# Two attention layers on 32x32 tiles of TensorE, with 32x32 block transposes on VectorE

## Chip, cores and metric

The kernel runs on one core of a Trainium2 chip. The metric is the device time in microseconds. The kernel before has a median of 1524.22 us over three runs (1521.26 to 1524.74).

## What is computed

128 sequences of 64 tokens with 128 features go through four layers, each with a context of the same shape:

```python
# layer 0: causal attention (key < query; row 0 is zero), 16 heads of 8
q, k, v = query @ Wq + bq, key @ Wk + bk, values @ Wv + bv     # split into heads
attn = softmax(where(j < i, q @ k.T / sqrt(8), -1e30)); attn[:, :, 0, :] = 0
x = layer_norm(query + (attn @ v) @ Wo + bo)
x = layer_norm(x + relu(x @ W1 + b1) @ W2 + b2)
# layer 1: the same heads, no mask, no norm
x = x + softmax(q @ k.T / sqrt(8)) @ v @ Wo + bo
x = x + gelu(x @ W1 + b1) @ W2 + b2
# layer 2: gated fusion with the pooled context, then layer norm
# layer 3: RMS norm, 16 heads of 64
x = x + softmax(split(normed @ wq) @ split(ctx @ wk).T) @ split(ctx @ wv) @ wo
```

All is float32. Some products are made in three passes of a rounded format instead: a matrix is held as `high`, its rounded copy, and `low`, the rest, and high x high, high x low and low x high are summed (`split_mm`).

## The kernel before, in words

The work is cut into 16 groups of 8 sequences (512 tokens). Features lie on the 128 partitions, tokens in the free dimension, so that a tile of a group is 128x512. One head of 8 features takes 8 partitions. `PLAN` lists, for each engine, the steps of a group with a place in time; `PLANS` has own lists for the first two and the last two groups. `program` shifts a group's list by `TURN` and merges all groups by these numbers. The numbers set an order and nothing else: each engine runs its steps in it, and `Signal` gives the semaphore value that a step waits for. Steps of neighbouring groups alternate therefore. `BANKS` names the PSUM bank of every tile (8 banks of 128x512), `EMPTIED_BY` the step that frees it.

Names of steps: `q`, `k`, `v` are projections. `S.l.u` are the scores of layer l (0 or 1) and quad u (4 sequences), in four banks, one for each strip t of 32 partitions. `max` takes the largest score of each row (VectorE), `shift` subtracts it (TensorE, with `negmax` as weights), `exp` is ScalarE's, `sum` and a reciprocal VectorE's, `norm` the multiplication by it on GpSimd. `PT` transposes the normed probabilities on TensorE in four blocks of 128x128 per strip (line 740, `cst,prob`), `probT` copies them out of PSUM on ScalarE (line 1031). `O` multiplies them with the values, `ctx` picks each head's own part out of `O`'s banks into `aT` (lines 1280 and 1287), `o` is the output projection and `attout` adds the residual.

A head has only 8 rows, while a tile of TensorE takes 32 rows or more. So operands are masked: `Qm` holds the queries twice, each copy with other heads set to zero (ScalarE, line 1014), `Km` the keys twice (VectorE, line 1243), `Vm` the values twice (VectorE, line 1254), and one matmul of `S` (32 rows, 128 columns of weights, 128 moving columns) gives four heads' scores, 16 matmuls per quad. `O` has 64x32 tiles, 32 matmuls of 128 moving columns per quad, in two banks.

`h` and `f` are the two products of the feed-forward part; `h` is plain float32 here. `lnT`, `stats`, `rstd`, `z`, `lnF`, `ln_out` are the norms (transposes at line 740 with `fT` or `z`), `y_gamma`, `y_beta`, `square`, `yn`, `yn_high`, `yn_low` lead from layer 2 to layer 3. Steps with a 3 belong to the last layer; its probabilities go through `PT3` and `prob3T`, also with `cst,prob` at line 740. `out` adds layer 3's result into `y`, the last step of a group on VectorE (line 1416); SP stores `y` and loads the next group.

In the profile all matmuls but the transposes are of line 731. A plain float32 matmul leaves two records.

```python
rows = slice(32 * t, 32 * t + 32)
last = mm(blocks[t][:, s // 2, :, s % 2, :], Qm[l][rows, b].rearrange("p a q -> p (a q)"),
          Km[l][rows, b], start=(l == 1 and s == 0))
```

## Time and profile before

| | |
|---|---|
| median of 3 runs | 1524.22 us (1521.26 to 1524.74) |
| profiled execution | 1523.22 us |
| its span | 1521.7 us |
| TensorE busy | 1418.5 us, 93% |
| VectorE busy | 1080.6 us, 71% |
| ScalarE busy | 977.0 us, 64% |
| GpSimd busy | 488.1 us, 32% |
| DMA | 20.02 MB, mean 13 GB/s |

The span goes from the first to the last instruction; 1.5 us of the execution lie around it. Busy times of an engine are shares of the span. A mean of one operation is its own duration; where operations of one kind follow each other, the next starts before the last has ended, so that the distance of two starts is shorter than the duration. In the timeline a row joins neighbouring operations of one kind.

### The profile page before, as it was taken

Reading aid. Unit: us, or ns where it says so; the run is one execution under the profiler, and the core shown is the slowest. Engines: PE = TensorE matmul, PEld = TensorE weight load, DVE = VectorE, ACT = ScalarE, POOL = GpSimd, SP = SyncE. Lnnn points to the kernel's source line nnn. Section 1 sums busy time; section 2 is a strip of 40 time slices with the busy share of each in tenths; the row PEclk is TensorE's granted clock in tenths of the full one; section 3 lists DMA queues with packets and bytes.
Section 4 is the critical chain, followed back from the end, with each engine's and each line's share of the span. In section 5 each row is a group of like instructions: output and inputs, shape, how many; then the busy total and the mean of one; then the engine's idle time right before and its main releaser. Section 6 shows DMA issues by size and latency. Waiting matters only on the chain.

```text
span 1521.7 us, 48865 instructions
## 1 busy us (share of the span) xinstructions
PE 1418.5 (93%) x20325; PEld 1030.3 (68%) x20325; DVE 1080.6 (71%) x2644; ACT 977.0 (64%) x1877; POOL 488.1 (32%) x522
## 2 busy tenths in 40 slices
PE   4779999999999999999999999999999999999987
PEld 3455766767676676767667676776767667676756
DVE  4558778677786867778676777867687785776743
ACT  2355767667676766767576676767667676665654
POOL 2132523315242341524224252332424233152402
PEclk9999999999999999999999999999999999999998
DMA  4000000000000000000000000000000000000000
GB/s 141 15 2 15 3 8 16 9 16 2 22 3 9 16 9 16 3 22 3 9 16 9 16 3 22 3 9 16 9 16 3 9 16 9 2 3 8 3 8 9
DMA packets 27798, 20.02 MB, mean 13 GB/s; under 512 B 1088, under 2 KB 27200, under 8 KB 27328
## 3 DMA queue, kind: packets, MB, share of 16 engines
q1 hardware_dynamic: 27584, 16.90, 3.8%
q8 instruction: 167, 2.74, 0.8%
q14 instruction: 47, 0.39, 0.1%
HBM read 12.70 MB, written 4.19 MB: 11 GB/s over the span
## 4 chain that ended last, share of the span: by engine, by line
PE 76%; DVE 10%; POOL 5%; ACT 4%; issue 4%; DMA 0%; SPq 0%; ACTq 0%; DVEq 0%
PE bank L731 63%; PE bank L740 13%; DVE negmax L1261 2%; POOL prob L1157 2%; DVE sums L1408 2%; ACT prob L1096 1%; POOL rstd L1144 1%; DVE z L1319 1%; ACT probT L1031 1%; DVE negmax L1402 1%; DVE stats L1305 1%; POOL prob L1137 1%; POOL var_eps L1141 1%; POOL w_low L1128 0%; DVE mv L1310 0%
## 5 line engine op out<-in xcount | busy, mean ns | idle before, releaser
L1137 POOL TENSOR_TENSOR prob<-prob,rinv 128x512 f32<-128x512 f32 x256 | 262.4, 1044 | 369.1 <-DVE rinv L1268 368.7
L740 PE MATMUL bank<-cst,prob 128*128 128x128 f32 x1536 | 221.5, 277 | 14.5 <-POOL prob L1157 9.6
L740 PEld LDWEIGHTS bank<-cst,prob 128*128 128x128 f32 x1536 | 173.9, 141 | 62.5 <-issue 32.7
L1031 ACT ACTIVATE probT<-bank 128x512 f32<-128x512 f32 x256 | 143.8, 598 | 110.3 <-PE bank L740 109.4
L1261 DVE TENSOR_REDUCE negmax<-bank 128x8 bf16<-128x512 f32 x256 | 159.0, 680 | 70.7 <-PE bank L731 70.6
L1157 POOL TENSOR_TENSOR prob<-prob,rinv 128x512 f32<-128x512 f32 x128 | 132.5, 1042 | 230.0 <-DVE rinv L1412 229.7
L1024 ACT ACTIVATE prob<-bank 128x512 f32<-128x512 f32 x256 | 142.0, 608 | 80.3 <-PE bank L731 80.0
L1266 DVE TENSOR_REDUCE sums<-prob 128x8 f32<-128x512 f32 x256 | 169.2, 661 | 12.9 <-ACT prob L1024 11.0
L731 PE MATMUL bank<-negmax,ident_b 128*128 128x512 bf16 x384 | 129.6, 389 | 14.1 <-DVE negmax L1261 8.3
L731 PE MATMUL bank<-wt,Q 128*128 128x128 f32 x1024 | 126.1, 277 | 0.0
L1096 ACT ACTIVATE prob<-bank,rms_rows 128x256 f32<-128x256 f32 x256 | 104.5, 483 | 30.8 <-PE bank L731 30.7
L731 PEld LDWEIGHTS bank<-wt,Q 128*128 128x128 f32 x1024 | 120.8, 192 | 4.4 <-issue 1.0
L731 PE MATMUL bank<-room,wt 128*128 128x512 f32 x256 | 123.3, 593 | 0.0
L1074 ACT ACTIVATE K<-bank 128x512 f32<-128x512 f32 x128 | 74.2, 605 | 51.4 <-PE bank L731 51.0
L1141 POOL TENSOR_TENSOR var_eps<-mv,ln_eps 128x4 f32<-128x4 f32 x48 | 15.0, 313 | 279.1 <-DVE mv L1310 279.1
L1402 DVE TENSOR_REDUCE negmax<-bank 128x8 bf16<-128x512 f32 x128 | 81.6, 659 | 30.1 <-PE bank L731 30.0
L1109 ACT ACTIVATE Q<-bank 128x512 f32<-128x512 f32 x128 | 71.8, 597 | 46.6 <-PE bank L731 46.6
L1280 DVE TENSOR_SCALAR half_ctx<-bank,cst,vec 128x126 f32<-128x126 f32 (+1 forms) x128 | 46.4, 402 | 75.8 <-PE bank L731 75.6
L731 PE MATMUL bank<-c_high,w_high 128*128 128x512 f32 x160 | 85.4, 534 | 10.8 <-POOL w_low L1128 9.4
L1408 DVE TENSOR_REDUCE sums<-prob 128x8 f32<-128x512 f32 x128 | 85.1, 665 | 10.6 <-ACT prob L1096 10.3
L1079 ACT ACTIVATE V<-bank 128x512 f32<-128x512 f32 x128 | 75.7, 598 | 24.8 <-PE bank L731 22.6
L1104 ACT ACTIVATE prob3T<-bank 128x512 f32<-128x512 f32 x128 | 73.7, 603 | 26.3 <-PE bank L740 25.2
(155 smaller groups left out, 2968.7 us busy)
## 6 DMA issues: line engine op xcount, KB each, us to landing
x_in<-in_x SPq DMA_DIRECT2D x16, 256.0 KB, 3.0
c_in<-in_ctx SPq DMA_DIRECT2D x16, 256.0 KB, 3.3
out<-y SPq DMA_DIRECT2D x16, 256.0 KB, 2.3
Q<-in_split_weights SPq DMA_DIRECT2D x1, 1536.0 KB, 9.1
wt<-in_weights SPq DMA_DIRECT2D x1, 1024.0 KB, 10.8
wt<-in_weights SPq DMA_DIRECT2D x1, 640.0 KB, 5.9
wt<-in_weights SPq DMA_DIRECT2D x4, 128.0 KB, 10.4
cst<-in_constants SPq DMA_DIRECT2D x1, 229.0 KB, 2.7
```

Source lines behind the costliest of these rows:

```text
L731: return nc.tensor.matmul(o, lhsT, rhs, start=start, stop=stop, skip_group_check=True)
L740: last = nc.tensor.transpose(o[:, k * P:(k + 1) * P], src(k), ident)
L1024: nc.scalar.activation(prob[l][:, t].rearrange("p c k -> p (c k)"), bank(g, "S", l, u, t)[:, :], ACT.Exp, scale=SCALE8).then_inc(exp_ready ...
L1031: nc.scalar.activation(probT[:, t].rearrange("p s q -> p (s q)"), bank(g, "PT", l, u, t)[:, :], ACT.Identity).then_inc(probT_ready.sem, 1)
L1079: nc.scalar.activation(V3[:, b // 2, b % 2].rearrange("p j d -> p (j d)"), bank(g, "v3", b)[:, :], ACT.Identity).then_inc(v3_ready.sem, 1)
L1096: last = nc.scalar.activation(prob3[:, m % 2, :, i, :].rearrange("p (t e) k -> p t e k", e=2)[:, :, e, :], bank(g, "S3", m, e)[:, 256 * i: ...
L1137: nc.gpsimd.tensor_tensor(pr, pr, ri, ALU.mult).then_inc(norm_ready.sem, 1)
L1157: nc.gpsimd.tensor_tensor(pr, pr, ri, ALU.mult).then_inc(norm3_ready.sem, 1)
L1261: nc.vector.tensor_reduce(negmax[l][:, t, :], bank(g, "S", l, u, t)[:, :].rearrange("p (c k) -> p c k", c=8), AX.X, ALU.max, negate=True). ...
L1266: nc.vector.tensor_reduce(sums[l][:, t, :], prob[l][:, t], AX.X, ALU.add).then_inc(sum_ready.sem, 1)
L1402: nc.vector.tensor_reduce(negmax3[:, m % 2, e, :], bank(g, "S3", m, e)[:, :].rearrange("p (c k) -> p c k", c=8), AX.X, ALU.max, negate=Tru ...
L1408: nc.vector.tensor_reduce(sums3[:, m % 2, 4 * h:4 * h + 4].rearrange("p j i -> p (j i)"), prob3[:, m % 2, 4 * h:4 * h + 4].rearrange("p j ...
```

## The change

- **Scores.** `Qm` is gone: `queries` holds the queries once. `Km` holds the keys four times, one copy for each head of a strip, with the keys of a sequence ordered by parity. A matmul of `S` has 32 rows and 32 query columns as weights and 256 moving columns, and its output goes to 32 partitions: 32x32 tiles, 32 matmuls per quad. The causal mask is laid out anew for it.
- **Probabilities.** `PT` and `probT` are gone. `turn` on VectorE transposes a strip, 128x512, in 32x32 blocks from SBUF to SBUF.
- **Output.** `V` holds the values once, without a mask. `O` has 32x32 tiles, 32 matmuls of 256 moving columns per quad, in four banks. `ctx` picks four heads instead of two, with eight operations instead of four.
- **Copies.** `km` and `vm` move from VectorE to ScalarE.
- **`h`** becomes a split product: `x_high` on ScalarE and `x_low` on GpSimd are new, the weights W1 are split in the beginning.
- **`yn`** is gone. `lnF` of layer 2 transposes `y`, after gamma and beta; `yn_high` reads PSUM.
- `PLAN`, `PLANS`, `TURN`, `TILES` and `BANKS` are new throughout.

```diff
@@ the order: two lines of it @@
-        S.0.0@342.4468 shift.0.0.3@346.9911 ...
-TURN = 89.7521
+        S.0.0@199.6828 shift.0.0.0@203.6223 ...
+TURN = 83.4887
@@ buffers @@
-        Qm = [room[l][:, 0:2 * TOK].rearrange("p (b a q) -> p b a q", b=GB, a=2) for l in range(2)]
-        Km = [room[l][:, 2 * TOK:].rearrange("p (b c k) -> p b c k", b=GB, c=2) for l in range(2)]
+        Km = [room[l][:, :].rearrange("p (b h k) -> p b h k", b=GB, h=QUAD) for l in range(2)]
+        queries = [sb(f"queries{l}", [P, GB, L]) for l in range(2)]
-        Vm = sb("Vm", [P, 2, GB // 2, 2, P])
+        V = sb("V", [P, 2, 2, 2, P])
-        probT = sb("probT", [P, QUAD, QUAD, P])
+        probT = sb("probT", [P, QUAD, 8, L])
@@ TensorE @@
-                    for s in range(QUAD):
-                        b = QUAD * u + s
-                        for t in range(QUAD):
-                            rows = slice(32 * t, 32 * t + 32)
-                            last = mm(blocks[t][:, s // 2, :, s % 2, :], Qm[l][rows, b].rearrange("p a q -> p (a q)"),
-                                      Km[l][rows, b], start=(l == 1 and s == 0))
+                    for n in range(2):
+                        for i in range(QUAD):
+                            b = QUAD * u + i
+                            for t in range(QUAD):
+                                rows = slice(32 * t, 32 * t + 32)
+                                last = mm(blocks[t][32 * i:32 * i + 32, :, n, :], queries[l][rows, b, 32 * n:32 * n + 32],
+                                          Km[l][rows, b], start=(l == 1 and n == 0))
...
-                elif kind == "PT":
-                    l, u, t = index
-                    pe.wait_ge(*norm_ready(g, l, u, t))
-                    pr = prob[l][:, t].rearrange("p c k -> p (c k)")
-                    transpose4(bank(g, "PT", l, u, t), lambda k: pr[:, k * P:(k + 1) * P]).then_inc(probT_filled.sem, 1)
                 elif kind == "O":
...
-                        pe.wait_ge(*probT_ready(g, l, u, t))
+                        pe.wait_ge(*turned(g, l, u, t))
...
                     for j in range(2):
-                        for k in range(2):
-                            for r in range(2):
-                                rows = slice(64 * r, 64 * r + 64)
-                                for t in range(QUAD):
-                                    cols = slice(32 * t, 32 * t + 32)
-                                    last = mm(bank(g, "O", l, u, r)[cols, j * P:(j + 1) * P],
-                                              Vm[rows, l, 2 * u + j, k, cols], probT[rows, t, 2 * j + k, :],
-                                              start=(j == 0 and k == 0))
+                        for i in range(QUAD):
+                            rows = slice(32 * i, 32 * i + 32)
+                            for t in range(QUAD):
+                                cols = slice(32 * t, 32 * t + 32)
+                                last = mm(where[i][cols, 0:2 * P], V[rows, u, j, l, cols], probT[rows, t, :, 32 * j:32 * j + 32],
+                                          start=(j == 0))
...
-                    mm(bank(g, "h", l, j)[:, :], w(f"W1_{l}", j * P), (x1T[0] if l == 0 else fT[1])[:, :])\
+                    split_mm(bank(g, "h", l, j)[:, :], w_split(f"W1_{l}", j * P), (x_high[:, :], x_low[:, :]))\
@@ ScalarE @@
+                    nc.scalar.activation(queries[l][:, :, :].rearrange("p b q -> p (b q)"), bank(g, "q", l)[:, :],
+                                         ACT.Identity, bias=v(f"bq{l}")).then_inc(qm_ready.sem, 1)
...
+                        nc.scalar.activation(w_high[:, rest], w_stage[:, rest], ACT.Identity).then_inc(high_rest, 1)
+                        act.wait_ge(split_last_loaded, 16)
+                        nc.scalar.activation(w_high[:, last], w1_stage, ACT.Identity).then_inc(high_last, 1)
+                elif kind == "km":
...
-                    for a in range(2):
-                        last = nc.scalar.activation(Qm[l][:, :, a, :], bank(g, "q", l)[:, :].rearrange("p (b q) -> p b q", b=GB),
-                                                    ACT.Identity, bias=bqm[:, l, a:a + 1], scale=c("m_a", a))
+                    for h in range(QUAD):
+                        last = nc.scalar.activation(Km[l][:, :, h, :].rearrange("p b (j k) -> p b j k", j=2), by_parity,
+                                                    ACT.Identity, bias=bkm[:, l, h:h + 1], scale=m_h[:, h:h + 1])
+                elif kind == "vm":
...
+                    nc.scalar.activation(V[:, u].rearrange("p j l f -> p (j l f)"), bank(g, "v", u)[:, :], ACT.Identity)\
...
                 elif kind == "exp":
+                    if u or g:
+                        act.wait_ge(*(turned(g, l, 0, t) if u else turned(g - 1, l, 1, t)))
...
+                elif kind == "x_high":
...
+                    nc.scalar.activation(x_high[:, :], (x1T[0] if l == 0 else fT[1])[:, :], ACT.Identity)\
@@ GpSimd @@
+                elif kind == "x_low":
+                    l, = index
+                    pool.wait_ge(*x_high_ready(g, l))
+                    nc.gpsimd.tensor_tensor(x_low[:, :], (x1T[0] if l == 0 else fT[1])[:, :], x_high[:, :], ALU.subtract)\
@@ VectorE @@
+                elif kind == "turn":
+                    l, u, t = index
+                    dve.wait_ge(*norm_ready(g, l, u, t))
+                    if (l, u, g) != FIRST_QUAD:
+                        dve.wait_ge(*ctx_filled(QUAD_BEFORE[l, u, g][2], *QUAD_BEFORE[l, u, g][:2], part=QUAD - 1))
+                    nc.vector.transpose(probT[:, t].rearrange("p c k -> p (c k)"), prob[l][:, t].rearrange("p c k -> p (c k)"))\
+                        .then_inc(turned.sem, 1)
...
+                    for h in range(QUAD):
+                        for d in range(2):
...
+                            if h == 0:
+                                dve.wait_ge(*ctx_filled(g, l, u, part=2 * d + 1))
+                                nc.vector.tensor_scalar(half, o, m_h[:, 0:1], v(f"bv{l}"), ALU.mult, ALU.add)\
+                                    .then_inc(half_ready.sem, 1)
+                                continue
+                            dve.wait_ge(*half_ready(g, l, u, part=2 * (h - 1) + d))
+                            if h < QUAD - 1:
+                                nc.vector.scalar_tensor_tensor(half, o, m_h[:, h:h + 1], half, ALU.mult, ALU.add)\
+                                    .then_inc(half_ready.sem, 1)
+                            else:
+                                at = QUAD * u + 2 * d
+                                nc.vector.scalar_tensor_tensor(aT[l][:, at:at + 2, q0:L], o, m_h[:, h:h + 1], half,
+                                                               ALU.mult, ALU.add).then_inc(ctx_ready.sem, 1)
```

How the order moves, at three places. First TensorE, around the `O` of the first quad of layer 1 in a group of the middle, before (`cst,prob` are transposes, `probT,Vm` is `O`, `room` alone is `S`):

```order
L731 MATMUL bank<-wt,Q 128x128 x8
L740 MATMUL bank<-cst,prob 128x128 x4
L731 MATMUL bank<-negmax,ident_b 128x512
L731 MATMUL bank<-prob3T,V 64x64 x32
L740 MATMUL bank<-cst,prob 128x128 x12
L731 MATMUL bank<-negmax,ident_b 128x512
L740 MATMUL bank<-cst,prob 128x128 x4
L731 MATMUL bank<-probT,Vm 32x128 x32
L731 MATMUL bank<-room 128x2x64 x16
```

The same place in the change (`probT,V` is `O`, `room,queries` is `S`):

```order
L728 MATMUL banks<-wt,Q 128x128 x8
L728 MATMUL banks<-negmax,ident_b 128x512 x2
L728 MATMUL banks<-probT,V 32x256 x32
L728 MATMUL banks<-wt,Q 128x128 x8
L737 MATMUL banks<-cst,prob 128x128 x8
L728 MATMUL banks<-prob3T,V 64x64 x32
L728 MATMUL banks<-room,queries 32x4x64 x32
```

Of the transposes only those of the last layer are left (two strips of four), and `O` now stands between products of the last layer.

Second VectorE, around the `ctx` of the same quad, before (line 1266 is `sum`, 1408 the last layer's, 1261 `max`):

```order
L1408 TENSOR_REDUCE sums<-prob 128x8
L1412 RECIPROCAL rinv<-sums 128x8
L1266 TENSOR_REDUCE sums<-prob 128x8
L1268 RECIPROCAL rinv<-sums 128x8
L1280 TENSOR_SCALAR half_ctx<-bank,cst,vec 128x128 x2
L1287 SCALAR_TENSOR_TENSOR aT<-bank,cst,half_ctx 128x2x64 x2
L1261 TENSOR_REDUCE negmax<-bank 128x8 x4
```

In the change (line 1273 is `sum`, 1425 the last layer's):

```order
L1273 TENSOR_REDUCE sums<-prob 128x8
L1275 RECIPROCAL rinv<-sums 128x8
L1419 TENSOR_REDUCE negmax<-banks 128x8 x2
L1282 STREAM_TRANSPOSE probT<-prob 128x512 x3
L1425 TENSOR_REDUCE sums<-prob 128x8
L1429 RECIPROCAL rinv<-sums 128x8
...
L1300 TENSOR_SCALAR half_ctx<-banks,m_h,vec 128x128 x2
L1305 SCALAR_TENSOR_TENSOR half_ctx<-banks,m_h,half_ctx 128x128 x4
L1309 SCALAR_TENSOR_TENSOR aT<-banks,m_h,half_ctx 128x128 x2
```

Transposes stand between the reductions, and four more operations between the first and the last of a `ctx`.

Third TensorE at the start of the program, before (rows from the `k` of the first group on; the second threesome is a `k3`):

```order
L731 MATMUL bank<-c_high,w_low 128x512
L731 MATMUL bank<-pooled,wt 128x8
L731 MATMUL bank<-c_high,w_high 128x512
L731 MATMUL bank<-c_low,w_high 128x512
L731 MATMUL bank<-c_high,w_low 128x512
L731 MATMUL bank<-causal_rows,causal_pick 128x8x32 x8
L731 MATMUL bank<-room 128x2x64 x16
```

In the change:

```order
L728 MATMUL banks<-c_high,w_high 128x512
L728 MATMUL banks<-c_low,w_high 128x512
L728 MATMUL banks<-c_high,w_low 128x512
L728 MATMUL banks<-causal_rows,causal_pick 128x4x64 x8
L728 MATMUL banks<-room,queries 32x4x64 x32
```

No `k3` stands ahead of the first `S`.

## Rows read from the trace of the kernel before

**Rows 1.** The page: span, and busy time of each engine.
```profile
span 1521.7 us, 48865 instructions
PE 1418.5 (93%) x20325; PEld 1030.3 (68%) x20325; DVE 1080.6 (71%) x2644; ACT 977.0 (64%) x1877; POOL 488.1 (32%) x522
```
**Rows 2.** Busy time by stretch: PE, PEld, DVE, ACT, POOL, then PEclk, DMA share, GB/s.
```profile
403.00:1301.00 898.00, 867.24 (x12691) 635.09 (x12690) 668.77 (x1621) 607.76 (x1168) 299.68 (x319) 1.00 0.04 11
```
**Rows 3.** Timeline of VectorE, the last step of groups 1 and 14: start, us.
```profile
200.15 0.69 DVE L1416 TENSOR_TENSOR y<-bank,y 128x512 f32<-128x512 f32 x1 [0.50 <-PE bank L731]
...
1371.23 0.69 DVE L1416 TENSOR_TENSOR y<-bank,y 128x512 f32<-128x512 f32 x1 [4.39 <-PE bank L731]
```
**Rows 4.** The page: the chain that ended last, by engine.
```profile
PE 76%; DVE 10%; POOL 5%; ACT 4%; issue 4%; DMA 0%; SPq 0%; ACTq 0%; DVEq 0%
```
**Rows 5.** Timeline of TensorE: one strip's transposes and what follows.
```profile
620.28 0.60 PE L740 MATMUL bank<-cst,prob 128*128 128x128 f32 x4
620.72 0.38 PE L731 MATMUL bank<-negmax,ident_b 128*128 128x512 bf16 x1
```
**Rows 6.** Timeline of TensorE: an `O`, an `S` and what follows.
```profile
624.63 1.15 PE L731 MATMUL bank<-probT,Vm 64*32 64x128 f32 x64 [0.34 <-ACT probT L1031]
625.71 1.17 PE L731 MATMUL bank<-room 32*128 32x128 f32 x32
626.82 0.66 PE L740 MATMUL bank<-cst,prob 128*128 128x128 f32 x4
```
**Rows 7.** Timeline of TensorE: a split product, then a plain one, of 512 columns.
```profile
601.93 0.39 PE L731 MATMUL bank<-yn_high,w_high 128*128 128x512 f32 x1
...
602.63 0.28 PE L731 MATMUL bank<-rms_own,cst 128*128 128x8 f32 x2
...
648.51 1.02 PE L731 MATMUL bank<-room,wt 128*128 128x512 f32 x2
649.38 0.60 PE L740 MATMUL bank<-cst,prob 128*128 128x128 f32 x4
```
**Rows 8.** Waits of TensorE from 403 to 1301 us: total, times, longest.
```profile
PE bank L740 <- POOL prob L1157: 6.4, 27, 0.3
...
PE bank L731 <- ACT probT L1031: 3.5, 10, 0.4
```
**Rows 9.** Groups of VectorE, whole span: busy us, mean ns, idle before.
```profile
L1243 DVE TENSOR_SCALAR room<-bank,vec,m_c 128x512 f32<-128x512 f32 x64 | 48.4, 797 | 5.1 <-PE bank L731 5.1
L1254 DVE TENSOR_TENSOR Vm<-bank,m_vc 128x512 f32<-128x512 f32 x64 | 41.0, 683 | 35.4 <-PE bank L731 35.4
L1327 DVE TENSOR_TENSOR room<-x1T,gv 128x512 f32<-128x512 f32 x16 | 18.3, 1142 | 0.5
L1380 DVE TENSOR_SCALAR ynT<-bank,yn_scale 128x512 f32<-128x512 f32 x16 | 12.9, 804 | 4.9 <-PE bank L740 4.8
```
**Rows 10.** Timeline of VectorE: a `ctx` of a quad, then four maxima.
```profile
625.87 0.73 DVE L1280 TENSOR_SCALAR half_ctx<-bank,cst,vec 128x128 f32<-128x128 f32 x2 [1.31 <-PE bank L731]
626.52 0.60 DVE L1287 SCALAR_TENSOR_TENSOR aT<-bank,cst,half_ctx 128x128 f32<-128x128 f32 x2
627.04 2.47 DVE L1261 TENSOR_REDUCE negmax<-bank 128x8 bf16<-128x512 f32 x4
```
**Rows 11.** Groups of ScalarE, whole span.
```profile
L1031 ACT ACTIVATE probT<-bank 128x512 f32<-128x512 f32 x256 | 143.8, 598 | 110.3 <-PE bank L740 109.4
L1014 ACT ACTIVATE room<-bank,bqm,cst 128x512 f32<-128x512 f32 x64 | 46.2, 773 | 18.9 <-PE bank L731 18.2
L1063 ACT ACTIVATE yn_high<-ynT 128x512 fp32r<-128x512 f32 x16 | 10.1, 630 | 11.8 <-DVE ynT L1380 11.8
```
**Rows 12.** Group of GpSimd, whole span.
```profile
L1137 POOL TENSOR_TENSOR prob<-prob,rinv 128x512 f32<-128x512 f32 x256 | 262.4, 1044 | 369.1 <-DVE rinv L1268 368.7
```
**Rows 13.** Timeline of TensorE: the first `k3`.
```profile
26.01 0.80 PE L731 MATMUL bank<-c_high,w_high 128*128 128x512 f32 x1 [9.41 <-POOL w_low L1128]
```

766 lines of the change are left out of this document (367 added, 399 removed), and 9 rows, old and new, of the table BANKS.

## Prediction

> **What bounds the kernel now.** I read the totals of the page first. TensorE is busy for 1418.5 of 1521.7 us, VectorE for 1080.6 [rows 1]. Then the stretches, since a share over the whole span mixes start, middle and end: from 403 to 1301 us TensorE is busy for 867.24 of 898 us (96.6%) at a granted clock of 1.00, VectorE for 74.5%, ScalarE for 67.7%, GpSimd for 33.4% [rows 2]. Next the distance between groups: the sum into `y` that closes a group starts at 200.15 and, thirteen groups later, at 1371.23, so a group takes 90.1 us [rows 3]. Per group this is 87.0 us of TensorE and 3.1 us in which it idles, 67.1 of VectorE, 61.0 of ScalarE, 30.1 of GpSimd. The chain of waits agrees: 76% of it is TensorE, 10% VectorE [rows 4]. So the kernel is a stream of sixteen groups behind one full engine. A microsecond of TensorE work taken out of a group is worth up to 15 us, since fifteen steps lie between sixteen groups; work on the others is free as long as they don't become late for TensorE, which obeys a written order.
>
> **What TensorE loses and gains.** The four transposes of one quarter of a quad take from 620.28 to 620.72, 0.44 us [rows 5]. There are 16 such quarters in a group (2 layers, 2 quads, 4 row strips), all removed: 7.0 us.
>
> The products of `h` change from plain to split form. A plain one of 512 columns (one matmul, two records) takes from 648.51 to 649.38, 0.87 us; a split one (three matmuls) from 601.93 to 602.63, 0.70 us [rows 7]. Eight per group save 1.4 us.
>
> The scores `S` and the products `O` are the unknown. The trace has no 32x32 tiles. It has `S` as 16 matmuls of 128 columns, four tiles side by side, 1.11 us; and `O` as 32 matmuls of 128 columns, eight tiles side by side, 1.08 us [rows 6]. Matmuls times columns over tiles is 512 in both, and both take the same time. Now each is 32 matmuls of 256 columns on sixteen tiles: 512 again. `O` already issues its 64 records in 1.08 us, so the number of instructions isn't new either. I take 1.1 us, no change. Bounds: below, nothing is won (512 columns through a tile remain); above, only eight tiles work side by side (2.2 us) or four (4.4 us). I am nearest to the `O` row, which shares the number of records, the 32 columns of each weight tile and the many tiles.
>
> Here a rule weighs against the change. The Trainium skill (TensorE: Matmul & The Clock Gate, "Measured speedup vs the span model") gives 3.07 for four row tiles and 10.6 for sixteen, not 16. Four tiles agree with the trace: sixteen matmuls of 128 columns are four of 0.87 us, 3.48, and took 1.11. By the page the new block would be sixteen times 0.87 over 10.6, an estimated 1.31 us.
>
> TensorE then needs 87.0 - 7.0 - 1.4 = 78.6 us per group.
>
> **VectorE.** Removed per group: the masked keys (48.4 us in all), the masked values (41.0) and `ynT` (12.9) [rows 9], over 16 groups 6.4 us. Added: 16 transposes of 128x512. No row has one. Other operations that stream 512 elements step by 0.62 us (four `negmax` in 2.47) [rows 10]; the slowest row of that size is the product into `room` at 1.14 us [rows 9]. I take 0.62, as the transpose has one input and no broadcast: 9.9 us. 0.62 to 1.14 is the range, so 9.9 to 18.2. Nothing speaks for less than 0.5 us.
>
> `ctx` has eight operations for each quad instead of four. Two `tensor_scalar` take 0.65 us (625.87 to 626.52), two `scalar_tensor_tensor` 0.52 [rows 10]. Before: 1.17. Now two and six: 0.65 + 6 x 0.26 = 2.2. Four quads: 4.2 us more. `yn_low` reads PSUM now, 0.1. Sum: 67.1 - 6.4 + 9.9 + 4.2 + 0.1 = 74.9 us (83.2 with slow transposes). VectorE goes from 74% to near 90% of a group and is the second full engine.
>
> **ScalarE and GpSimd.** ScalarE loses 143.8 us of `probT` and 46.2 of masked queries [rows 11], 11.9 per group. It gains ten bias copies by the latter's row (0.72 each, two `qm` and eight in two `km`), two of `vm` by the former's (0.56) and two `x_high` (0.63): 9.6. So 58.7 us, no bound. What waits behind the four copies of a `km` is `S`; in the table `km.1` stands some twenty us before `S.1.0`, so this is hidden but in the first group. GpSimd gains two `x_low` by the row of its 512-element product (1.03) [rows 12]: 32.2 us.
>
> **Moves.** In the order of TensorE the run of `cst,prob` between the `negmax` and the `O` is gone; `O` waits for four transposes of VectorE in its place. They stand behind sums of layers 3 and 1 and ahead of a `ctx`, so a late `norm` on GpSimd now holds up VectorE, where before it held TensorE: TensorE idled 6.4 us for the last layer's `norm` and 3.5 for `probT` in the whole stretch [rows 8]. The second goes. A quad's latency falls by 0.44 + 0.56 and rises by 0.62 + 1.05; `x_high` and `x_low` put 1.7 us ahead of each `h`. In the middle neighbouring groups cover this. `exp` must now wait until the same strip of the quad before is turned, which the order has ahead of it. SP's queue gets one load more, at the start, and its waits stay.
>
> **The period.** 78.6 plus the old 3.1 of idle is 81.7. VectorE's free time would shrink from 23.0 to under 7 us there, and its work comes in bursts (four maxima, four sums, four transposes), each 2.5 us and more, in a fixed order. With a third of the slack, I let TensorE's idle nearly double, by 2.5, and take 84.2, where VectorE has 9 us free: no growth would need perfect cover, and growth by 8.4 would mean that VectorE's bursts are covered by nothing. This is the softest step. It keeps 5.9 of the 8.4 us.
>
> **Start and end.** TensorE idles 9.41 us until 26.01, for the low halves of the weights of `k3`, ahead of the first `S` [rows 13]. Now the first `S` stands ahead of any `k3`; it waits for ScalarE, which rounds these weights (and the new 1024 columns) ahead of `km`. I take 5 us of the 9.4 as won. The longer chains of the first and last group (two `h`, four `ctx`) cost 4 us.
>
> **Sum.** 15 x 5.9 = 88.5; plus 5, less 4: 89.5 us. From the profiled execution's 1523.2 us this gives 1433.7, so **1434 us**. The median of the runs shown, 1524.2, is 1 us above that execution, inside their spread of 3.5.
>
> **Rivals.**
> 1. *Sixteen tiles lose more than eight.* Each of the eight blocks (`S` and `O`) takes 1.3 us instead of 1.1, as extra staggering of 16 starts; 1.6 per group, 25 in all: 1459. Against: four and eight tiles cost the same [rows 6]. Chance 0.10. (This is the page's 10.6 as a mechanism; by it the time is the same 1459.)
> 2. *VectorE becomes the bound.* Transposes at the 1.14 us of the slowest row make 83.2 us of work; with its short gaps and a few waits the group takes about 87.5. Gain 15 x 2.6 + 1 = 40: 1483. For: no row of a transpose, and 90% is already little slack. Chance 0.13.
> 3. *Slower: column tiles of one row strip don't run side by side.* Then a block of `S` or `O` goes by eight or four. With eight, 2.2 us: 78.6 + 8.8 + 3.1 = 90.5 per group, about 1529. With four, 4.4 us: 105 + 3.1 = 108, about 1793. It decides once a block takes over 1.1 + 5.9/8 = 1.84 us. For: the four strips read four streams each, which no row shows. Against: `O` has four column tiles and two row tiles, with a stream of their own each, at the full rate. Chance 0.09.
> 4. *The change doesn't take the transposes out.* Excluded: the order has none left, and 32 transposes by VectorE between the reductions.
>
> **How the numbers follow.** The forecast has 0.66. Its own range goes from 1400 (idle nearly unchanged; all of it unchanged gives 1396) to 1465 (5 us more idle than taken, less than the 8.4 removed). Rivals 1 and 2 lie at 1459 and 1483; reaching to 1488 leaves out rival 3, part of rival 2 and a little at both ends of the forecast: 2 in 10. 0.3% is 4.6 us, about what a measurement of this kernel can tell from none. Faster by more: 0.66 + 0.10 + 0.11 = 0.87; the same, 0.03, from a bad rival 2 or a mild rival 3; slower 0.10, rival 3 and what I haven't thought of.
>
> **What would show it.** Right: no `cst,prob` but the last layer's 512 transposes; blocks `banks<-room,queries` and `banks<-probT,V` of 1.1 us from start to next start; `probT<-prob` near 0.62 to 0.68 us; groups 84 us apart; TensorE still over 92% busy and VectorE near 89%. Wrong: a block over 1.8 us, a transpose over 1.1, or chains in which VectorE has a third; `O` idle behind `turn`, with GpSimd's `prob` as what VectorE waits for, would say that the idle was mis-sized and not the work.

## The result, and the profile after it

The changed kernel takes 1526.32 us (median of 20 runs, 1522.39 to 1530.63), the kernel before 1523.13 on the same chip (1516.29 to 1525.42): ratio 1.0024, 95% interval 1.0013 to 1.0035. That is no difference, or one of a quarter of a per cent in the wrong direction, where I had forecast 1434 us. The profiled execution has a span of 1523.1 us. Two runs further down stand apart from the others of their kernel, one of six of `few_before` (1519.41 us, with a granted clock of 0.94 where the others have 0.99) and one of four of `placed_few2` (2531.77 us); the time given for `placed_few2` and the second ratio given for `few_before` leave them out.

The page of the changed kernel, the stretch from 403 to 1301 us (PE, PEld, DVE, ACT, POOL, PEclk, DMA share, GB/s) and the chain of waits answer to [rows 1, 2, 4]:

```profile
span 1523.1 us, 51571 instructions
PE 1359.0 (89%) x21477; PEld 926.2 (61%) x21477; DVE 1197.4 (79%) x3005; ACT 928.3 (61%) x1782; POOL 519.9 (34%) x555
...
PE 62%; DVE 20%; ACT 9%; issue 7%; POOL 2%; DMA 0%; SPq 0%; DVEq 0%; ACTq 0%
```
```profile
403.00:1301.00 898.00, 828.66 (x13402) 567.67 (x13401) 740.73 (x1853) 573.19 (x1105) 318.14 (x340) 1.00 0.04 11
```

TensorE did get less to do: busy for 828.66 us of the stretch instead of 867.24. But it idles for 69.3 us instead of 30.8, and the groups pass no faster. VectorE and ScalarE are where I had put them. In the chain VectorE, ScalarE and `issue` have taken what TensorE lost.

The sixteen sums into `y` of the changed kernel start at 189.92, 287.02, 375.43, 464.56, 553.47, 642.38, 731.88, 820.79, 911.13, 1001.26, 1092.84, 1184.69, 1276.69, 1367.10, 1447.94 and 1519.33 us. So the first group is 10.2 us earlier than before [rows 3], the next thirteen take 90.55 us each instead of 90.08, 6.1 us more in all, and the last two take 152.2 us instead of 146.8 (1371.2 to 1518.1). The three sum to 1.3 us. A short start is won, and everything else is lost again.

The blocks themselves, on the timeline of TensorE (start, duration, idle before), for [rows 6] (the transposes of [rows 5] are gone):

```profile
657.01 1.48 PE L728 MATMUL banks<-probT,V 32*32 32x256 f32 x64
658.42 0.50 PE L728 MATMUL banks<-c_high,w_high 128*128 128x512 f32 x1
```
```profile
642.84 1.48 PE L728 MATMUL banks<-probT,V 32*32 32x256 f32 x64
644.25 0.40 PE L728 MATMUL banks<-causal_rows,causal_pick 32*128 32x256 bf16 x8
644.58 1.38 PE L728 MATMUL banks<-room,queries 32*32 32x256 f32 x51
646.70 0.66 PE L728 MATMUL banks<-room,queries 32*32 32x256 f32 x13 [0.74 <-issue]
```

An `O` takes 1.41 us to the next start, not 1.1. And in this group, where `O`, the causal mask and `S` follow each other, TensorE stops for 0.74 us in the middle of `S`, after 51 of its 64 records, with nothing it waits for. Its waits in the stretch (total, times, longest) answer to [rows 8]. The first line is of the kernel before, the others of the changed one:

```profile
PE bank L731 <- issue: 9.2, 19, 1.6
PE banks L728 <- issue: 23.9, 33, 1.3
PE banks L728 <- ACT prob3T L1120: 9.2, 11, 1.1
PE banks L728 <- DVE negmax L1268: 5.7, 21, 0.5
PE banks L728 <- DVE aT L1309: 5.6, 9, 1.2
PE banks L728 <- DVE probT L1282: 5.0, 6, 1.0
```

Summed by what ended them, before and after, these lists have 9.2 and 23.9 us of `issue`, 3.9 and 19.9 us of waits for ScalarE, 5.8 and 17.5 for VectorE, 6.9 and 2.4 for GpSimd. So `issue` is over a third of the new idle time, and the rest is waiting for ScalarE and VectorE. Behind `issue` the largest single growth is that of ScalarE's `prob3T`, from 0.4 to 9.2 us.

The groups of the other engines that my sum had bounded by [rows 9 to 12] (busy, mean ns | idle before):

```profile
L1282 DVE STREAM_TRANSPOSE probT<-prob 128x512 f32<-128x512 f32 x256 | 162.4, 681 | 9.8 <-POOL prob L1151 9.5 <-issue 0.2
L1305 DVE SCALAR_TENSOR_TENSOR half_ctx<-banks,m_h,half_ctx 128x126 f32<-128x126 f32 (+1 forms) x256 | 71.3, 342 | 0.0
L1020 ACT ACTIVATE room<-banks,bkm,m_h 128x512 f32<-128x512 f32 x128 | 88.9, 775 | 24.5 <-PE banks L728 24.5
L1155 POOL TENSOR_TENSOR x_low<-fT,x_high 128x512 fp32r<-128x512 f32 x16 | 20.4, 1278 | 89.0 <-ACT x_high L1052 89.0
```

A table of my own splits TensorE's time better than busy shares do. For each step of TensorE (an `O`, a `shift`, an `h`) I took the time from the end of the last record of the step before to the end of its own. The tenth percentile of a kind of step is its length when nothing holds it up; its sum over a group is TensorE's work, what is left of the stretch is gaps. (`h` answers to [rows 7], the transposes `PT` to [rows 5].)

```
                        S.0   S.1   O     h     PT    work/group   gaps/group   of which pieces over 0.25 us
before                  1.22  1.10  1.09  0.86  0.44  82.6         7.4          3.9
changed                 1.75  1.42  1.42  0.68  -     77.4         12.7         9.8
```

So the question for the experiments: the work fell by 5.2 us a group (not by 8.4), and the gaps grew by 5.3. Why both?

### The profile page after: what moved, and what is told of

Read it like the earlier page. It is cut to its first block, busy times and chain, and to the rows that moved or that the text cites. A ratio compares the mean times of both kernels' runs of the same rounds, so it can differ in the third digit from the quotient of the medians.

```text
span 1523.1 us, 51571 instructions
## 1 busy us (share of the span) xinstructions
PE 1359.0 (89%) x21477; PEld 926.2 (61%) x21477; DVE 1197.4 (79%) x3005; ACT 928.3 (61%) x1782; POOL 519.9 (34%) x555
## 3 DMA queue, kind: packets, MB, share of 16 engines
q8 instruction: 175, 2.87, 0.8%
## 4 chain that ended last, share of the span: by engine, by line
PE 62%; DVE 20%; ACT 9%; issue 7%; POOL 2%; DMA 0%; SPq 0%; DVEq 0%; ACTq 0%
PE banks L728 57%; PE banks L737 5%; DVE negmax L1268 3%; DVE half_ctx L1305 2%; DVE probT L1282 2%; DVE half_ctx L1300 2%; DVE z L1341 1%; ACT prob L1112 1%; DVE sums L1273 1%; ACT prob3T L1120 1%; DVE negmax L1419 1%; ACT L1062 1%; ACT prob L1036 1%; POOL rstd L1163 1%; DVE aT L1309 1%
## 5 line engine op out<-in xcount | busy, mean ns | idle before, releaser
L1036 ACT ACTIVATE prob<-banks 128x512 f32<-128x512 f32 x256 | 142.8, 600 | 95.5 <-PE banks L728 94.9
L1268 DVE TENSOR_REDUCE negmax<-banks 128x8 bf16<-128x512 f32 x256 | 160.3, 684 | 46.5 <-PE banks L728 46.4
L1282 DVE STREAM_TRANSPOSE probT<-prob 128x512 f32<-128x512 f32 x256 | 162.4, 681 | 9.8 <-POOL prob L1151 9.5
L728 PE MATMUL banks<-negmax,ident_b 128*128 128x512 bf16 x384 | 127.9, 387 | 18.4 <-DVE negmax L1268 14.6
L1112 ACT ACTIVATE prob<-banks,rms_rows 128x256 f32<-128x256 f32 x256 | 103.9, 483 | 42.5 <-PE banks L728 41.7
L728 PEld LDWEIGHTS banks<-wt,Q 128*128 128x128 f32 x1024 | 121.7, 192 | 7.9 <-issue 4.9
L728 PE MATMUL banks<-wt,Q 128*128 128x128 f32 x1024 | 125.9, 276 | 0.0
L728 PE MATMUL banks<-room,wt 128*128 128x512 f32 x256 | 118.6, 596 | 6.6 <-ACT room L1062 6.6
L728 PE MATMUL banks<-probT,V 32*32 32x256 f32 x4096 | 97.1, 392 | 18.6 <-DVE probT L1282 13.7
L728 PE MATMUL banks<-room,queries 32*32 32x256 f32 x4096 | 100.4, 393 | 13.7 <-ACT room L1020 5.3
```

Source lines behind the costliest of these rows:

```text
L728: return nc.tensor.matmul(o, lhsT, rhs, start=start, stop=stop, skip_group_check=True)
L1036: nc.scalar.activation(prob[l][:, t].rearrange("p c k -> p (c k)"), bank(g, "S", l, u, t)[:, :], ACT.Exp, scale=SCALE8).then_inc(exp_ready ...
L1112: last = nc.scalar.activation(prob3[:, m % 2, :, i, :].rearrange("p (t e) k -> p t e k", e=2)[:, :, e, :], bank(g, "S3", m, e)[:, 256 * i: ...
L1268: nc.vector.tensor_reduce(negmax[l][:, t, :], bank(g, "S", l, u, t)[:, :].rearrange("p (c k) -> p c k", c=8), AX.X, ALU.max, negate=True). ...
L1282: nc.vector.transpose(probT[:, t].rearrange("p c k -> p (c k)"), prob[l][:, t].rearrange("p c k -> p (c k)"))\
```

## The experiments

Each kernel was timed together with the kernel before, on one chip. Its ratio to that is given; the changed kernel's own stands at 1.0024, and "against the changed kernel" means the difference of the two ratios.

**1. What a tiled block costs by itself.** TensorE alone repeats a block between full matmuls. Each has 512 columns on every tile; tiles, matmuls and order differ.

```
sections = {            # row tiles, column tiles, columns, matmuls per tile, order
  "col16": (4, 4, 256, 2), "row16": same, rows inner, "dia16": same, diagonals,
  "wide16": (4, 4, 512, 1), "narrow16": (4, 4, 128, 4),
  "col8": (2, 4, 256, 2), "narrow8": (2, 4, 128, 4), "row4": (4, 1, 256, 2), "one": (1, 1, 256, 2)}
```

> TensorE alone (the reference's computation is left out: the kernel only copies a piece of x to the output): after warming up, ten repetitions each of a block of small fp32 matmuls with a full 128x128 by 512-column matmul between them. Every tiled block puts 512 columns on each of its tiles, so the array's own need is the same for all of them. Theory 'feed': a block on 16 tiles is set by the number of its matmuls. In the changed kernel a block of 32 matmuls of 256 columns took 1.42 us; here col16, row16 and dia16 (32 matmuls, three orders) take 1.35 to 1.5 us all three, narrow16 (64 matmuls of 128 columns) over 2.2 us, wide16 (16 matmuls of 512) 0.95 to 1.1, col8 (16 matmuls on 8 tiles, 64 rows each) 0.9 to 1.05, narrow8 (32 of 128 on 8 tiles, the block of the kernel before) 1.08 to 1.3. Rival 'tiles share something': the array runs 16 tiles slower whatever the number of matmuls: wide16 takes 1.35 to 1.5 like col16, and the order matters (one of row16, col16 and dia16 is over 10% faster).

The timeline, a block and the full matmul behind it, by turns `col16`, `wide16`, `col8`, `narrow8` (the names lose their number):

```profile
26.25 1.50 PE L67 MATMUL banks<-m_col,w_col 32*32 32x256 f32 x64
27.68 1.13 PE L67 MATMUL banks<-sep_m,sep_w 128*128 128x512 f32 x2
...
98.20 1.14 PE L67 MATMUL banks<-m_wide,w_wide 32*32 32x512 f32 x32
99.27 1.12 PE L67 MATMUL banks<-sep_m,sep_w 128*128 128x512 f32 x2
...
163.03 1.09 PE L67 MATMUL banks<-m_col,w_col 64*32 64x256 f32 x32
164.05 1.12 PE L67 MATMUL banks<-sep_m,sep_w 128*128 128x512 f32 x2
...
181.87 1.16 PE L67 MATMUL banks<-m_narrow,w_narrow 64*32 64x128 f32 x64
182.96 1.13 PE L67 MATMUL banks<-sep_m,sep_w 128*128 128x512 f32 x2
```

Start to start: 1.425 us for sixteen tiles in all three orders, 1.07 for the same sixteen tiles in half the matmuls (`wide16`), 1.02 for half the matmuls on eight tiles, 1.09 for the kernel before's form, 1.08 for four row tiles, 2.69 for 64 matmuls on sixteen tiles (`narrow16`). That last one isn't the price of the tiles alone: nine of its ten blocks hold a stop of 0.2 to 0.85 us of the kind that experiment 7 shows, and the first, which has none, took 1.83, where I had expected over 2.2. `one`, two full matmuls of 256 columns, takes 0.86. Sixteen tiles do work side by side and their order is indifferent; the theory "feed" holds. The single records of a `col16` block show how: 33 start within 0.46 us, the next at 0.65, and from there one every 16.6 ns to 1.12 us, and the last still has its 256 columns to do. In `narrow8`, the form that I had reasoned from, the last record starts at 0.89 us and lasts 0.27 instead of 0.37 us, so that a late last one costs less. The Trainium skill (TensorE: Matmul & The Clock Gate, "Measured speedup vs the span model") has 10.6 for sixteen tiles, by which I had estimated 1.31 us. Here sixteen blocks of 0.864 us over 1.425 give 9.7, and over the 1.071 of the longer matmuls 12.9: the number isn't one of the tiles alone.

**2. VectorE's transposes cut short, tiles halved, and both.**

```
-  nc.vector.transpose(probT[:, t] (512 columns), prob[l][:, t] (512 columns))      # turn_short: the first 32
-  S, O: 4 row tiles x 4 column tiles, rows 32 * i : 32 * i + 32, 32 matmuls        # blocks8
+  S, O: 2 row tiles x 4 column tiles, rows 64 * r : 64 * r + 64, 16 matmuls
```

> The changed kernel with VectorE transposing only the first 32 of the 512 columns of each probability tile (the other columns of probT keep a constant: the outputs of the first two layers are not the reference's). VectorE does some 0.6 us less for each of 16 transposes a group, about 9.5 us of 74 a group. Theory A (TensorE's own work and its instruction supply took the gain, VectorE is only a small part): the waits of TensorE that VectorE ended were about 17 us of the 898 us looked at, so at most 28 us go, probably 8 to 20: 1506 to 1518. Theory B (VectorE's added load is what took the gain, since it delays TensorE everywhere in a fixed order): 45 us or more go, 1480 or less. If nothing changes (over 1521), VectorE's 681 ns transposes cost nothing.

> The changed kernel with S and O of the first two layers issued as 16 matmuls on 8 tiles of 64x32 instead of 32 on 16 tiles of 32x32, same 256 moving columns each and same columns per tile, VectorE untouched (the sums then run over wrong rows: outputs of these layers are not the reference's). Theory A (the 16-tile blocks are held by the feeding of their 32 matmuls): each of 8 blocks a group goes from 1.42 to 0.95 to 1.1 us, so 0.3 to 0.45 us by 128 blocks is 40 to 58 us, and half the tiled matmuls' instructions less also takes away some of the issue stalls: 1465 to 1490. Theory B (another engine has become the limit): TensorE's saving turns into waits on VectorE and ScalarE, less than 15 us goes: 1510 or more.

> turn_short and blocks8 together. Theory A: the two add up, about the sum of the two single gains within 8 us; both on different terms of TensorE's time: 1450 to 1480. Theory B: turn_short alone gains most and blocks8 adds under 15 us to it. If VectorE is the limit only once TensorE is shorter, both gains together are over 15 us more than their sum.

| kernel | us | ratio to before, 95% interval | against the changed kernel |
|---|---|---|---|
| `turn_short` | 1514.29 | 0.9953 (0.9934 to 0.9972) | -0.7%, 11 us |
| `blocks8` | 1493.92 | 0.9821 (0.9795 to 0.9847) | -2.0%, 31 us |
| `both` | 1478.54 | 0.9714 (0.9682 to 0.9747) | -3.1%, 47 us |

Theory A holds, though `blocks8` gained 31 us where I had put 40 to 58. Taking nearly 10 us of 74 a group from VectorE gives 0.7 us a group; the effects add up (11 + 31 = 42 against 47). Halving the matmuls takes 2.8 us a group of work away (77.4 to 74.7 in the table's measure), and 2.0 of it reach the end. The rest went into gaps: TensorE's waits for VectorE's `ctx` (`aT`) grew from 5.6 to 16.4 us in the stretch.

```profile
403.00:1301.00 898.00, 819.99 (x11119) 560.16 (x11125) 757.50 (x1900) 592.94 (x1148) 320.99 (x346) 1.00 0.04 10
...
PE banks L728 <- issue: 16.9, 26, 1.5
PE banks L728 <- DVE aT L1309: 16.4, 30, 1.4
```

**3. A new order.** I wrote a replay of the program, with step lengths and latencies between engines read from the changed kernel's trace. It gave the changed kernel's order 1484 us, and a search over the tables found orders with less. Only `PLAN`, `PLANS` and `BANKS` differ.

> The changed kernel with its steps placed anew once more (only the tables PLAN, PLANS and BANKS differ: which step comes after which on each engine, and which PSUM bank a tile takes; the instructions are the same). The order was searched with durations read from the changed kernel's trace: for each step of TensorE the time from the end of the step before to its own end, for the other engines start to start, and for every wait the time from the releaser's end. The same replay gives the changed kernel's own order 1484 us (39 us under its 1523 span: it knows nothing of instruction-supply stalls) and this one 1449. Theory 'order' (TensorE's work did fall by 5.2 us a group, 82.6 to 77.4, and the gaps in the placed order took it back, 7.4 to 12.7): 1480 to 1500. Rival 'supply' (the added gaps come with the number and density of instructions, wherever the steps stand): within 10 us of the changed kernel, 1515 or more.

1524.47 us, ratio 1.0003 (0.9986 to 1.0020), 0.2% under the changed kernel: a miss, and by the terms above the rival "supply" had it. (A second order of the same search, `placed_b`, has steps of several engines that wait for each other in a ring; it never ends and has no time.) By my replay, of which no trace is kept, part of the miss was my own: the table's numbers were cut to four decimals, by which close steps changed places, and the order as it ran has 1473 in the replay. But the gaps were 12.6 us a group as before. They had only moved: TensorE's waits for ScalarE's `prob3T`, ahead of `O3`, grew from 9.2 to 18.8 us in the stretch, and `issue` fell only from 23.9 to 20.1. The replay's error was largest at the first `S3` of every group, 0.77 us. That led to experiment 5.

**4. The `h` step undone.**

```
-  split_mm(h, w_split(W1), (x_high, x_low))     three matmuls
+  mm(h, w(W1), x1T[0] or fT[1])                 one fp32 matmul; no x_high, x_low
```

> The changed kernel with the h step undone: W1 is again one fp32 weight and h one fp32 matmul of 512 columns (0.858 us of TensorE instead of 0.680), and x_high and x_low are not made (ScalarE 0.63 and POOL 1.27 us less, twice a group). Theory A (the split gives what TensorE saves, 8 times 0.18 us a group): 1.4 us by 16, 18 to 25 us slower than the changed kernel, 1543 to 1550. Theory B (TensorE waits for POOL's x_low, about 0.9 us before h.1 and 0.24 before h.0 in each group, which undoes most of it): within 10 us of the changed kernel, 1518 to 1535.

1533.09 us, ratio 1.0062 (1.0042 to 1.0082), 0.4% or 6 us above the changed kernel. So the split brings 0.36 us a group of the 1.4 that TensorE saves. The size is theory B's, its reason is not: the first `h.1`, which stands behind an `S`, ends 0.77 us late without any `x_low`, and 0.80 with it. In eight of the ten groups of the stretch TensorE stands idle ahead of it until `ctx` has ended on VectorE. `BANKS` gives this `h` a bank that held the `O` just before the `S`, and `ctx`, with eight operations instead of four, empties it too late. The changed kernel (TensorE, then VectorE), and `plain_h`:

```profile
466.77 1.49 PE L728 MATMUL banks<-room,queries 32*32 32x256 f32 x64
468.87 0.50 PE L728 MATMUL banks<-x_high,w_high 128*128 128x512 f32 x1 [0.60 <-DVE aT L1309]
...
468.21 0.60 DVE L1309 SCALAR_TENSOR_TENSOR aT<-banks,m_h,half_ctx 128x126 f32<-128x126 f32 x2
```
```profile
471.36 1.13 PE L727 MATMUL banks<-fT,wt 128*128 128x512 f32 x2 [0.60 <-DVE aT L1301]
```

No run gives this `h` another bank or `ctx` fewer operations.

**5. Waits that are already met.** The kernel writes a wait for every tile and bank, 278 a group: nine ahead of an `O` (before: seven), eighteen ahead of the first `S3`, sixteen of which name eight copies each of `K3` and `Q3`. Not each is an instruction of its own, as the first expectation below has it: the trace has 1913 waiting instructions in TensorE's queue, 120 a group, and nine of them ahead of the first `S3`; the other waits ride on these or on weight loads. The edit keeps waits back until the next matmul and issues of each semaphore only the highest value, and none that an earlier wait covers:

```
+  def wait_ge(self, sem, value):
+      self.kept[id(sem)] = (sem, max(value, self.kept.get(id(sem), (sem, 0))[1]))
+  def flush(self):                                  # ahead of every matmul
+      for sem, value in self.kept.values():
+          if value > self.seen.get(id(sem), 0): self.wait(sem, value); self.seen[id(sem)] = value
```

> The changed kernel, same order and same matmuls, but TensorE issues no wait that an earlier one on the same semaphore already covers, and of several on one semaphore only the last: each wait is a separate instruction in TensorE's queue (278 waits a group in the changed kernel, 9 before each O block, 18 before the first S3 block, where 0.77 us a group is lost in each group beyond what the replay explains). Theory 'issue' (waits that are met still cost their issue where the queue can't run ahead, before the tiled blocks above all): 0.8 to 1.5 us a group less, 1500 to 1513. Rival (waits that are met cost nothing; the 0.77 us is the wait itself, for the last K3 or Q3): within 5 us of the changed kernel, 1520 to 1530.

> The same edit of TensorE's waits in the kernel before (302 waits a group; 7 before each O block, 18 before the first S3 block). If the issue of waits is a cost that the change did not add, this kernel gains about what few_after gains (1500 to 1513, ratio of the two within 0.4%). If it is 16-tile blocks, with their nine waits and 32 matmuls, that make it a cost, this kernel gains less than half of that: 1515 or more.

| kernel | us | ratio to before, 95% interval |
|---|---|---|
| `few_after` | 1491.18 | 0.9798 (0.9775 to 0.9822) |
| `few_before` | 1503.48 | 0.9891 (0.9857 to 0.9925) |

`few_after` gains 2.3%, 34 us, more than I had expected, with 394 waiting instructions left. `few_before` gains 1.1% by its six runs, and 1.2%, 19 us, by five (ratio of the means 0.9875), which is neither as much as `few_after` nor less than half of it. So met waits cost time in both kernels, and nearly twice as much in the changed one. Without them the change is worth about 0.8% (0.9798 to 0.9875). The first `S3` of a group in the changed kernel, then in `few_after`:

```profile
689.12 0.60 PE L737 MATMUL banks<-cst,z 128*128 128x128 f32 x4
690.35 2.10 PE L728 MATMUL banks<-K,Q 64*64 64x64 f32 x128 [0.63 <-issue]
```
```profile
679.21 0.60 PE L756 MATMUL banks<-cst,z 128*128 128x128 f32 x4
679.74 2.10 PE L746 MATMUL banks<-K,Q 64*64 64x64 f32 x128
```

From the start of the transposes to the first score it is 1.23 us with eighteen waits (nine instructions) and 0.53 with three (one instruction). In `few_after` the idle put down to `issue` falls from 23.9 to 9.6 us.

**6. The search again, with the waits gone.** The replay with `few_after`'s durations missed its span by 11 us only, and this time the tables' numbers were kept as searched.

> few_after with its steps placed anew (the tables PLAN, PLANS and BANKS alone): the order was searched with durations taken from few_after's trace. The replay gives few_after 1481 us (measured span 1492) and this order 1448. With the waits' issue gone the replay leaves out only 0.5 us a group, so this time it should hold. Theory 'order' (TensorE's 11.5 us of gaps a group in few_after are a matter of the order): 1455 to 1470. Rival (the gaps move elsewhere again, as in placed_a): 1485 or more.

> The same with another result of the same search, 1449 us in the replay. Theory 'order': 1455 to 1470, within 8 us of placed_few. Rival: 1485 or more.

> The order of placed_few with TensorE's waits as in the changed kernel (278 a group, met ones too). If the waits' issue is a cost of its own, 25 to 40 us above placed_few as few_after stands to the changed kernel: 1485 to 1505. If in this order the waits fall where the queue can run ahead: within 10 us of placed_few. If over 1510, the order is worth nothing without the waits' removal, as placed_a was.

| kernel | us | ratio to before, 95% interval |
|---|---|---|
| `placed_few` | 1477.13 | 0.9723 (0.9696 to 0.9750) |
| `placed_few2` | 1480.31 | 0.9746 (0.9711 to 0.9780) |
| `placed_many` | 1514.02 | 0.9954 (0.9936 to 0.9971) |

The order gives another 0.75%, 11 us, a third of the 33 that the replay promised, so both orders missed their range above. The waits cost 2.3% in this order too: 37 us between `placed_many` and `placed_few`. `placed_many` came out over 1510, where I had meant to call the order worth nothing without the waits' removal. That reading was too strong: it is 0.7% under the changed kernel, which has the same waits, so the order is worth as much with them as without. `placed_few` leaves nothing of the computation out and beats both kernels, by 2.8% and 3.0%. TensorE is busy for 858.94 of its 898 us, and `issue` is down to 3.5:

```profile
403.00:1301.00 898.00, 858.94 (x13973) 591.52 (x13971) 768.43 (x1922) 598.27 (x1164) 328.25 (x353) 1.00 0.04 11
...
PE banks L778 <- ACT prob3T L1173: 10.1, 20, 0.7
PE banks L778 <- DVE negmax L1321: 3.7, 18, 0.2
PE banks L778 <- issue: 3.5, 7, 1.4
```

**7. The price of a met wait, by itself.** TensorE alone repeats pairs of blocks, full or 16-tile, with 0 to 18 met waits between them.

> TensorE alone (the reference's computation is left out: only a piece of x is copied to the output). Pairs of blocks, a full 128x128 fp32 matmul of 512 columns or a 16-tile block of 32 matmuls of 256 columns, with 0, 1, 2, 4, 9 or 18 waits between them on a semaphore that has long been reached; eight repetitions each, the period of a repetition read. Theory 'issue': a met wait costs some 20 to 60 ns of TensorE's queue. Behind a full matmul (857 ns for two records) the queue runs ahead and hides up to about nine waits; in front of and behind tiled blocks, whose records are issued until shortly before their end, it hides few: nine waits cost 0.2 to 0.5 us a pair, 18 waits 0.6 to 1.1 us. That is what few_after's 33 us need: about 2 us a group over 60 waits removed. Rival: the waits cost nothing (every period the same within 0.05 us), and few_after's gain is of another kind, for example the shorter instruction stream.

Period of a pair, median of seven, from the records. The number is of waits as written; the trace has one waiting instruction for each two of them (none for one, four for nine, nine for eighteen):

```
waits              0      1      2      4      9      18
full, full         1.717  1.717  1.717  1.717  1.717  1.717
full, tiled        2.481  2.481  2.481  2.481  2.481  2.481
tiled, full        2.481  2.481  2.481  2.481  2.481  2.886
tiled, tiled       3.469  3.471  3.740  3.695  3.903  4.346
```

Behind a full matmul of 512 columns eighteen met waits are free. Behind a tiled block nine are still free if a full matmul follows; eighteen cost 0.405 us, 22 ns for each written wait if all of them count and 45 if the first nine stay free. The first `S3` of a group isn't among these pairs: it stands behind four short transposes and `full, tiled` has no cost at all, so that place rests on `s3_waits` below. Between tiled blocks the single periods spread too much to price a few waits (3.46 to 4.01 us without any, once the stops have begun); only with eighteen is the median outside that spread. The surprise is the first column: two 16-tile blocks in a row take 3.47 us, not 2 x 1.425. The timeline of `tiled, tiled`, first without waits and then with four, shows why:

```profile
379.66 2.74 PE L59 MATMUL banks<-m_tiled_tiled_0w,w_tiled_tiled_0w 32*32 32x256 f32 x128 [0.72 <-issue]
383.13 2.75 PE L59 MATMUL banks<-m_tiled_tiled_0w,w_tiled_tiled_0w 32*32 32x256 f32 x128 [0.72 <-issue]
...
470.62 2.87 PE L59 MATMUL banks<-m_tiled_tiled_4w,w_tiled_tiled_4w 32*32 32x256 f32 x127 [0.47 <-issue]
474.50 2.87 PE L59 MATMUL banks<-m_tiled_tiled_4w,w_tiled_tiled_4w 32*32 32x256 f32 x127 [1.02 <-issue]
478.49 2.92 PE L59 MATMUL banks<-m_tiled_tiled_4w,w_tiled_tiled_4w 32*32 32x256 f32 x127 [1.12 <-issue]
```

After every 128 records without waits, and 127 with four, TensorE stands for 0.5 to 1.3 us. With weight loads and waiting instructions that is 256 instructions from stop to stop in both. The instruction stream comes in pieces of that size: the changed kernel's page has 175 for 2.87 MB, 16 KB each, and the trace has 44869 instructions in TensorE's queue, 175.3 times 256 (before: 167 pieces, 42749 instructions, 167.0 times 256). Stops end 3.3 to 4.0 us apart here, so when a piece is used up sooner, TensorE stands. That it waits for the next piece is my reading; no run fed the same blocks by another way. The Trainium skill (Runtime: NRT & Kernel Launch, "Instruction fetch mechanics") has such blocks of 16 KiB, 256 instructions each, which the sequencer fetches itself, and calls the cost of crossing a boundary mostly hidden. The size agrees (2.87 MB over 175, stops every 256); hidden it isn't where tiled blocks follow each other.

```profile
q8 instruction: 175, 2.87, 0.8%
```

**8. By place, or by number?** Met waits could cost because of where they stand, or because they lengthen this stream. `padded` is `few_after` with three met waits ahead of each `k3`, `v3`, `q3` and `f`; `s3_waits` is the changed kernel with

```
-  for p in range(PAIRS): if m == 0: pe.wait_ge(*k3_ready(g, p)); pe.wait_ge(*q3_ready(g, p))
+  if m == 0: pe.wait_ge(*k3_ready.whole(g)); pe.wait_ge(*q3_ready.whole(g))
```

> few_after with 96 met waits a group put back (as many as it had lost, 95), but elsewhere: three ahead of each k3, v3, q3 and f product, which are full matmuls that mostly stand behind full matmuls, where m_waits showed 18 waits to be free. Theory 'place' (a met wait costs only where TensorE's queue has no lead, in front of and behind tiled blocks): within 6 us of few_after, 1487 to 1497. Theory 'stream' (instructions come to TensorE in pieces, and any added instruction makes the pieces run out sooner, wherever it stands): most of the 33 us come back, 1510 to 1525.

> The changed kernel with one place alone cleaned: the first S3 block waits twice (for the last of the eight K3 and of the eight Q3 of the group) instead of sixteen times. 14 waits a group less of 278. Theory 'place': the transposes ahead of it start 1.23 us before it in the changed kernel and 0.53 in few_after, so 0.7 us a group go, 8 to 12 us: 1513 to 1518. Theory 'stream': 14 of the 95 instructions that gave 33 us, 5 us or less: 1519 to 1523.

`padded`: 1496.89 us, 0.9824 (0.9805 to 0.9843); the waits put back cost 0.26%, 4 us, and the two intervals overlap. `s3_waits`: 1518.49 us, 0.9961 (0.9950 to 0.9972); 14 waits a group less give 0.63%, 10 us. Both have to be weighed by instructions. The pages count 50897 for `padded`, 50052 for `few_after`, 51459 for `s3_waits` and 51571 for the changed kernel. So the 96 waits a group of `padded` brought back only 845 of the 1519 instructions that were gone; by number, 56% of 34 us would have come back, 19 us. And `s3_waits` took out 112, seven a group, by number 2.5 us. The place decides.

## Why the prediction was wrong, step by step

**What bounds the kernel: right, and read too simply.** A stream of groups behind TensorE it is; `blocks8` and `few_after` show that taking from TensorE pays. But "a microsecond of TensorE work taken out of a group is worth up to 15 us" needs the idle to stay, and each edit kept only a part: 2.0 of 2.8 us with `blocks8`, 0.36 of 1.4 with the `h` split, nothing of the change's 5.2.

**Transposes removed, 7.0 us: right.** Sixteen of 0.44.

**`h`, 1.4 us: right as work** (0.86 to 0.68, eight times); 0.36 us of it arrive.

**`S` and `O`, no change: the first step that failed.** I took 1.1 us a block "nearest to the `O` row, which shares the number of records" and wrote that the number of instructions wasn't new. Measured is 1.42 for six of the eight and 1.75 (with the mask) for the two `S` of layer 0, before 1.09 to 1.22. Sum per group: 12.0 us instead of 9.0, 3.0 more. The row had the records but not their length. Rival 1 had this mechanism at 1.3 us and with 1.6 us per group; it was nearly twice that.

**VectorE, 74.9 us: right.** 740.73 of 898 us by the period of 90.55 is 74.7; a transpose takes 681 ns, of which 0.59 to the next start, where I took 0.62. Rival 2 falls, and `turn_short` prices the transposes at 0.7 us a group. The added operations of `ctx` (I had 4.2 us a group) no run takes out. ScalarE (57.8 for 58.7) and GpSimd (32.1 for 32.2) too; `x_low` took 1.27 us, not 1.03.

**The period: the second step that failed, by as much.** I let the idle grow by 2.5 us and had called it the softest step. In the page's measure it grew by 3.8 (30.8 to 69.3 in 898 us); in the measure of step lengths the gaps grew by 5.3, and with 5.2 of work saved that is the whole result. I had reasoned from VectorE's slack alone. The experiments divide it otherwise. Of the 85 us that the gaps took (5.3 by 16), 15 are what met waits cost the changed kernel beyond what they cost the kernel before (34 less 19, experiment 5); VectorE's transposes hold about 11 us at most (`turn_short`, which also takes out what they would cost in any order); the order holds 11 more that I could find (experiment 6). The rest, over half, isn't settled. The lists of waits say of what kind the whole growth is: in the 898 us `issue` grew by 14.7 us, waits for ScalarE by 16.0 and waits for VectorE by 11.7, while those for GpSimd shrank by 4.5. So waiting for other engines is three fifths of the growth, and that for ScalarE, which I had put down as no bound, is the largest part. One place of it is plain, the `h.1` that waits for the longer `ctx` (experiment 4), 5.4 us in the stretch. Stops inside tiled blocks are another part, by my reading of experiment 7 for want of instructions: those of over 60 ns were 9 with 9.3 us in the whole run before, and 17 with 22.5 after. But no run takes either away by itself.

**Start and end.** The start gave 10.2 us (I took 5). The end cost 5.4 us in the last two groups (I took 4).

**Rival 3** (tiles not side by side) falls with 1.42 us a block and its deciding point of 1.84. The outcome came in through no rival of mine: work saved and gaps grown by the same amount. I had no case in which TensorE's queue is the limit, though [rows 8] are cut from a list whose first line, `issue` with 9.2 us, I didn't weigh. And my range took each failure by itself; here both came, 3.0 us a group from the blocks and 2.8 from the gaps (5.3 less the 2.5 allowed), by 15 some 87 of the 92 us that I was off by.

## What to carry to other kernels

Price a tiled block by the number of its matmuls and by how long each of them lasts, and measure it by itself: columns over tiles is a lower bound. Before taking work from an engine that is busy for 97% of the time, look at what its queue does: waits that are long met, and stretches with many small instructions. Leaving out TensorE's covered waits gave 1.2% and 2.3%, more than the new tiling did.

When an engine gets more operations on a tile, look for who waits for that tile's bank, not only at its busy share.

An order written for other lengths loses what a change saves. Place it again with measured lengths, and replay the tables as they are written out.

## What the runs showed of the hardware that I had not expected

- A 16-tile fp32 block of 32 matmuls of 256 columns takes 1.425 us in any order, 1.07 with 16 matmuls of 512, and with 64 of 128 it takes 1.83 without a stop, 2.69 with one.
- Eighteen met waits (nine instructions) between a 16-tile block and a full matmul cost 0.405 us, nine (four instructions) cost nothing; behind a full fp32 matmul of 512 columns eighteen cost nothing.
- Two 16-tile blocks in a row take 3.47 us instead of 2.85, with a stop of 0.5 to 1.3 us every 256 instructions (128 matmul records and their weight loads), and TensorE's 44869 instructions of the changed kernel come in 175 pieces of 16 KB, 256 to a piece.
- Between the end of one operation and the start of the one that had waited for it lie nearly always about the same times: 32 ns from ScalarE to VectorE, 36 from TensorE to ScalarE, 34 from GpSimd to VectorE, 79 from VectorE to GpSimd, 146 from VectorE or GpSimd to a transpose or split matmul of TensorE (medians of the changed kernel's records). With these my replay gave 1481 us for `few_after`'s span of 1492.
